# Attention over 120 keys in two layers: masked keys in place of masked queries, and values and sums of a head from one product, joined by VectorE's block transposes

## The reference, cut to what matters

```python
q, k, v = layernorm(x) @ Wq, ctx @ Wk, ctx @ Wv      # split in 16 heads of 8
scores = q . k / sqrt(8) + mask or bias
out = softmax(scores) @ v                            # [128, 16*8]
x = x + tanh(g) * (out @ Wo)
```

## Time and profile before

| | |
|---|---|
| median of 3 runs | 961.47 us (961.18 to 963.21) |
| the profiled execution | 967.42 us |
| its span | 965.7 us |
| mean granted TensorE clock | 0.911 of full speed |
| TensorE busy | 772.4 us, 80% of the span |
| VectorE busy | 689.2 us, 71% |
| GpSimd busy | 614.8 us, 64% |
| ScalarE busy | 494.7 us, 51% |

### The profile page before, as it was taken

One profiled execution on the slowest core, in us unless ns is written; L12 is line 12 of the kernel. 1 busy time (PEld: TensorE's weight loads), 2 busy tenths in 40 slices (PEclk: granted clock), 3 DMA queues, 4 the chain that ended last, 5 costly groups with the idle time before them and its releaser, 6 DMA issues. The chain is left out here.

```text
span 965.7 us, 30722 instructions
## 1 busy us (share of the span) xinstructions
PE 772.4 (80%) x9843; PEld 590.3 (61%) x9843; DVE 689.2 (71%) x2096; ACT 494.7 (51%) x1719; POOL 614.8 (64%) x1114
## 2 busy tenths in 40 slices
PE   3999999999957998369999999999930278888770
PEld 2777777777743666247777778778720146657560
DVE  3788888888866664157888888888869756775334
ACT  2777777777740212047877877777710032342320
POOL 4888666666643676467877877777410266777772
PEclk9999999999977999579999999999965579999995
DMA  6111222222113333134333443343200225665567
GB/s 173 60 64 63 85 76 73 73 73 73 72 60 94 101 103 99 46 99 132 122 111 125 138 129 113 126 138 122 78 15 0 65 49 139 180 183 160 163 187 217
DMA packets 98743, 100.83 MB, mean 104 GB/s; under 512 B 24510, under 2 KB 76076, under 8 KB 98658
## 3 DMA queue, kind: packets, MB, share of 16 engines
q1 hardware_dynamic: 88306, 88.25, 29.4%
q0 software_dynamic: 6656, 9.66, 3.7%
q10 hardware_dynamic: 3696, 1.84, 0.7%
HBM read 60.84 MB, written 44.17 MB: 109 GB/s over the span
## 5 line engine op out<-in xcount | busy, mean ns | idle before, releaser
L558 ACT ACTIVATE P<-bank,mx 128x120 f32<-128x120 f32 x1024 | 278.1, 436 | 12.9 <-DVE mx L849 12.4
L460 PE MATMUL bank<-ident,P 128*120 128x128 f32 x1024 | 166.4, 285 | 12.2 <-ACT P L558 9.1
L849 DVE TENSOR_REDUCE mx<-bank 128x4 f32<-128x480 f32 x256 | 150.3, 649 | 18.2 <-PE bank L447 15.3
L460 PEld LDWEIGHTS bank<-ident,P 128*120 128x120 f32 x1024 | 106.0, 137 | 58.0 <-issue 29.1
L1695 POOL DMA_INDIRECT xg<-token_rows,tokens x64 | 66.3, 1036 | 71.0 <-DVE tokens L1749 52.1
L476 PE MATMUL bank<-PT,Vb 120*32 120x128 f32 x2048 | 105.9, 279 | 0.0
L476 PE MATMUL bank<-PT,headcols 120*32 120x128 f32 x2048 | 102.8, 273 | 0.0
L437 PE MATMUL bank<-bp,identr 128*128 128x480 f32 x256 | 87.3, 427 | 0.0
L1705 POOL DMA_INDIRECT expert_sums<-y,sum_rows x64 | 72.2, 1129 | 23.4 <-issue 18.9
L660 POOL TENSOR_TENSOR Qm<-qf,qmask 128x512 f32<-128x512 f32 x64 | 67.4, 1054 | 27.5 <-ACT qf L542 26.7
L624 POOL TENSOR_SCALAR rs<-mv 128x1 f32<-128x1 f32 x128 | 28.9, 226 | 84.6 <-DVE mv L831 84.3
(11 more groups left out here) (245 smaller groups left out, 1819.3 us busy)
## 6 DMA issues: line engine op xcount, KB each, us to landing
expert_sums<-zeros SPq DMA_DIRECT2D x32, 512.0 KB, 3.4
choice_rows<-zeros SPq DMA_DIRECT2D x32, 384.0 KB, 2.4
yrows<-choice_rows SPq DMA_DIRECT2D x32, 384.0 KB, 3.2
XT<-expert_sums SPq DMA_DIRECT2D x16, 512.0 KB, 6.6
XS<-expert_sums SPq DMA_DIRECT2D x16, 512.0 KB, 6.1
w<-in_w13T SPq DMA_DIRECT2D x8, 704.0 KB, 4.1
token_rows<-payload SPq DMA_DIRECT2D x32, 128.0 KB, 1.7
ctx<-in_ctxT SPq DMA_DIRECT2D x64, 60.0 KB, 1.9
```

The lines of the kernel that those rows point to most:

```text
L460: mm = nc.tensor.transpose(TB[r % 2][0:KV, S * j:S * j + S], t.P[:, r, j, :], t.ident[:])
L558: e = nc.scalar.activation(t.P[:, r, j, :], heads(SC[r])[:, j, :], ACT.Exp, bias=t.mx[:, G * r + j:G * r + j + 1], scale=-1.0)
L849: ve.tensor_reduce(t.mx[:, G * r:G * r + G], heads(SC[r]), AX.X, ALU.min).then_inc(ev.mins, 1)
```

## The change

1. Masked keys. GpSimd now makes four copies of the keys (`head_keys`, tile `Km`, 128x480) and not of the queries, and the queries are the weights. One product per row group gives all four heads of the group, 480 columns wide. ScalarE copies `Kf` ahead of `qf`.
2. Values and sums together. A head's weights are nine columns: its 8 values and a column of ones, in a slot of 16. Two heads (32 columns) fill one row group of PSUM, so values and sums of 16 heads stand in `pv_ps`, now 256 columns. `headcols` and its products are gone.
3. VectorE turns `pv_ps` in blocks of 32x32 (`turn_values`) into `ov`, where the sums of the 16 heads are 16 columns; inverts these 16 (`invert_sums`), multiplies (`divide`, both inputs in SBUF) and turns the result back (`turn_back`) into `oT`.
4. The statistics of the batch three ahead are split in two helpers, and with the choice (layer 0) or the addition of the experts' rows (layer 1) put between the four steps of 3.
5. `BEHIND` is 4 in both layers: while layer 0 drains, its choice comes one step earlier, with the second norm.

```diff
-AHEAD, BEHIND = 4, (5, 4)
+AHEAD, BEHIND = 4, 4
...
+def with_ones(v):
+    return v.rearrange("p v g (r x) -> p (v g r) x", x=48)
+def draining(i, ahead=0):
+    return isinstance(i, int) and i >= B + 1 - ahead
...
             def scores(b, u):
-                for j in range(G):
-                    for r in range(G):
-                        rows = slice(32 * r, 32 * r + 32)
-                        mm = nc.tensor.matmul(heads(SC[r])[:, j, :], t.Qm[rows, u, j, :], t.Kf[rows, u, :],
-                                              start=False, stop=(j == G - 1))
+                for r in range(G):
+                    rows = slice(32 * r, 32 * r + 32)
+                    nc.tensor.matmul(heads(SC[r]), t.qf[rows, u, :], t.Km[rows, u, :, :],
+                                     start=False, stop=True).then_inc(ev.scores, 1)
...
-                for out, col in ((pv_ps, None), (sum_ps, t.headcols)):
-                    for j in range(G):
-                        w = t.Vb[0:KV, v, j, 32 * r:32 * r + 32] if col is None else col[0:KV, r, :]
-                        mm = nc.tensor.matmul(out[32 * j:32 * j + 32, :], w,
-                                              t.PT[0:KV, r, S * j:S * j + S], start=(r == 0 and col is None),
-                                              stop=(r == G - 1), skip_group_check=True)
+                for j in range(G):
+                    mm = nc.tensor.matmul(pv_ps[32 * j:32 * j + 32, S * (r // 2):S * (r // 2) + S],
+                                          t.Vb[0:KV, v, 2 * j + r // 2, 32 * (r % 2):32 * (r % 2) + 32],
+                                          t.PT[0:KV, r, S * j:S * j + S], start=(r % 2 == 0), stop=(r % 2 == 1),
+                                          skip_group_check=True)
...
-            def head_queries(n, w):
-                nc.gpsimd.tensor_tensor(t.Qm[:, w, :, :], t.qf[:, w, :].unsqueeze(1).broadcast_to([D, G, S]),
+            def head_keys(n, w):
+                nc.gpsimd.tensor_tensor(t.Km[:, w, :, :], t.Kf[:, w, :].unsqueeze(1).broadcast_to([D, G, KV]),
...
-            def invert_sums(p, u, c):
+            def turn_values(p, c):
                 dve.wait_ge(ev.pv, G * (p + 1))
-                c.note(ve.reciprocal(t.rsum[:], sum_ps))
-            def normalise(p, u, c):
+                used(dve, ev.out, p)
+                c.note(ve.transpose(t.ov[:].rearrange("p (q h x) -> p h q x", h=2, x=32), pv_ps))
+            def invert_sums(c):
+                c.settle()
+                c.note(ve.reciprocal(t.rsum[:].unsqueeze(2), sixteen(t.ov)[:, :, DK:DK + 1]))
+            def divide(c):
+                c.settle()
+                c.note(ve.tensor_tensor(t.on[:].rearrange("p (g d) -> p g d", d=DK), sixteen(t.ov)[:, :, 0:DK],
+                                        t.rsum[:].unsqueeze(2).broadcast_to([128, 16, DK]), ALU.mult))
+            def turn_back(p, u, c):
                 c.settle()
                 used(dve, ev.proj, p - 1)
-                scaled = ve.tensor_tensor(t.oT[:, u, :], pv_ps, t.rsum[:], ALU.mult)
-                scaled.then_inc(ev.out, 1)
+                ve.transpose(t.oT[:, u, :], t.on[:]).then_inc(ev.out, 1)
```

143 lines of the change are left out of this document (88 added, 55 removed).

## The result

| | before | changed |
|---|---|---|
| device time, median | 962.34 us (961.18 to 971.79, 4 runs) | 940.41 us (935.60 to 943.52, 4 runs) |
| profiled execution | 967.42 us, span 965.7 | 940.70 us, span 938.9 |
| TensorE's granted clock over the span, share of 2.4 GHz | 0.911 | 0.903 |

The ratio of the times is 0.9744, 95% interval 0.9702 to 0.9785: the changed kernel is 2.6% faster. The forecast was 928.5 us in a range of 914 to 944, so the time lies inside the range, 12 us above the forecast. The two profiled executions differ by 26.7 us, the sum of the prediction was 33.

The account below looks back on a forecast made before the run. Layer 0 was taken as bound by two near-equal loops closing in the scores (ScalarE's exponentials; sums to `oT`), layer 1 by VectorE's string; 11.9 + 17.2 + 1 + 3 = 33 us, from the 961.5 us median 928.5, range 914 to 944.

Parts of the forecast that it names:

- Layer 0: Layer 0's step: with `oT` early, TensorE waits for ScalarE; 7.50 us against 7.94, saving 0.44 x 27 = 11.9 us.
- scores to turn: Scores stage on TensorE: four products of 480 columns take 0.95 us to the next turn, before 1.10; -0.15 us.
- The four VectorE instructions: VectorE's transpose, reciprocal, division, transpose back: 0.45, 0.24, 0.29, 0.30 us, sum 1.28 against 1.25 removed; only waiting changes.
- VectorE's string: Layer 1: VectorE's run of instructions bounds the step; shortening it saves 0.66 us per step, to 8.15, 17.2 us in all.
- the "better" rival: Layer 1: experts' addition never meets GpSimd's long product, period falls to GpSimd's 7.85; sum 41, 920 us; chance 0.06.
- GpSimd is behind both and neither ends last: 0: Small parts: `head_keys` waits for `Kf`, `qf` follows one instruction later; GpSimd follows both, neither ends last; cost 0.
- The ends: Ends of the layers: nine further steps save about 0.35 each, 3 us; layer 0's dropped last step 1 us.
- The drain: End of layer 0: loses its last step, but remaining steps carry more in line; between 0 and 2.7, taken 1 us.
- the first rival: Layer 1 gives little: division and transposes contend with GpSimd, period stays at 8.6, 942 us; chance 0.17.
- The passes of a wide product: Scores: second passes block the next row group, five passes, 2.1 us; layer 0 step 8.65, 974 us; chance 0.05.
- dear: VectorE's transposes cost 0.96 us per 128 columns, +2.1 us on VectorE, 1028 us; chance 0.02.
- The clock: TensorE, with 0.9 us less per step, falls to 1.2 GHz at times, losing part of the gain; 0.02, shared with other causes.

Follow-up runs that it names:

- the added copy: The changed kernel with one more 128x512 ScalarE copy per step of both layers, its result unread; ratio 1.0034 to the kernel before.
- the second set of products back: The changed kernel with a second set of four products per group, weights zero, giving TensorE back the removed products; 949.28 us, 0.9831 of the kernel before.

## Why the prediction was right, and where it was off

**Layer 0: right, and for the reason given.** The prediction had 7.50 us, with ScalarE late next; the loop runs at 7.50, and ScalarE's idle time fell from 1.70 to 1.25 us as said. The single terms were a little off and cancel: scores to turn 1.02 and not 0.95; from a turn to the end of that step's last exponentials it is 6.11 us as before (180.76 to 184.65 + 2.22 = 186.87); and to the last mask 0.05 and not 0.15. That ScalarE's part of the loop has no slack is shown by the added copy, which arrives in full. Of the 0.48 us per step the masked keys make 0.06 to 0.08 (two experiments, 0.15 predicted), and the sums product that is gone 0.10. What is left, about 0.3, I put down to the earlier `oT`, from transposes and a narrow reciprocal; no run takes these back alone, so that part is argued.

**The four VectorE instructions: right.** Predicted 0.45, 0.24, 0.29 and 0.30 us, measured 0.441, 0.243, 0.274 and 0.311. The Trainium skill (VectorE: DVE Perf Modes, The three transpose paths) gives 311 ns for a 128x128 transpose in bf16; the trace has the same 311 ns, although the data here are full precision. VectorE did not get less work, and the gain lies in the waits: with the four in a row layer 1 gives back 0.32 of its 0.53 us.

**Layer 1: the mechanism half right, the end wrong.** The step that failed is the one that ran the whole layer along VectorE's string to 8.15 us. The string did shrink as worked out: transpose to next copy is 553.39 - 551.62 = 1.77 us, against a predicted 1.85. But the period stopped at 8.25, because another loop is longer than what is left of the string. I had read it in layer 0 and not worked it out for layer 1: from the exponentials' start at 548.89 to their end at 553.95 ScalarE has 5.06 us, then come 0.19 to the bias, 0.61 for its two passes, 1.02 for the scores, 0.75 to the copy and 0.59 to the next exponentials at 557.11, together 8.22. That is layer 0's loop with a bias in two passes and slightly longer small parts. Four experiments show it: a third transpose on VectorE costs nothing, taking 0.4 us off VectorE gives nothing, 0.50 us more on ScalarE cost 0.51, and scores that take 0.08 us longer cost 0.06. No run lengthened GpSimd's string. Against the forecast 0.13 us per step are missing: 0.53 over the sixteen periods, where I had 0.66. From first to last residual it is -15.2 us, where 17.2 and some of the ends' 3 had been promised.

Even that much owes something to luck. I worked the 0.66 out from one step of 8.65 us, of the kind of which three in four are. Those fell from 8.58 on the mean to 8.21, by 0.37. The fourth fell from 9.71 to 8.49, by 1.22: in it the addition of the experts' rows took 1.23 us before (at 605.61, where the steps before and behind have 0.60) and takes 0.48 now. That is what the "better" rival had described, and it made up for part of what the string did not give.

**"GpSimd is behind both and neither ends last: 0": wrong at one place, right in the rest.** The keys' product is ready 0.5 us before the scores in layer 1 (554.28 against 554.75), and GpSimd then idles 0.60 us (up to 555.72). But in steps 6 and 7 it also clears `xp`, and the scores then stand for 2.14 us with the clock down behind them. The step that takes 11.21 us had taken 9.52 before, so the fault was there in the kernel before (a wait of 1.46 us with the clock at 1.00) and grew by 1.7 us. With the second set of products back the step takes 9.88 at a clock of 1.00, so about 1.2 us of the growth go with the clock and the rest with the longer wait. I had read one step of each layer, not the outlier among the 31. It eats 3.5 us of the changed kernel (11.21 - 7.75).

**The ends: 3 + 1 us, too much.** The drain was to give 1 us since it has a step less; it costs 1 us, since each remaining step has more in line, which the prediction named and took too cheaply. Beside the gap before, 288.6 - 276.0 = 12.6 us from last residual to `tile_count`, the changed kernel has 13.1. How much of the 3 us for the ends came can't be told from the step at 80 us and the long fourth steps; both together are in the sum below.

**The rivals.** Contention on the division, the first rival, is there but small: the median is 0.274 us, and only two of 64 take longer than 0.35 (0.64 and 0.83). So layer 1 gave less than forecast, as that rival had it, but not for its reason. The addition of the experts' rows got out of it, 0.311 us at the median after 0.594, as the "better" case had hoped. In layer 0 the choice (L944) moved into it instead: 0.160 us before, now

```profile
L944 DVE TENSOR_TENSOR sel<-marked,biased x32: 182/406/501, 60.2 to 275.4; 128x64 f32<-128x64 f32 x32
```

because it now meets GpSimd's masked product, for a shape half as wide: the 23 that overlap with `Km`'s row have a median of 0.41 us, and of the nine others eight take 0.18 to 0.23. It costs nothing there, since VectorE has slack. The Trainium skill (GPSIMD Engine Reference, Specifications, the entry on SBUF interfaces) names contention with VectorE instructions that have two SBUF inputs, and these rows agree. The passes of a wide product do not stand in line: eight passes take 1.09 us. The transposes, at 0.44 and 0.31 us, are not dear either. The clock, for which I saw little, cost about 1.2 us: it was down for some 3.4 us behind the wait at 80 us. Otherwise it was down in the attention layers only as they start (layer 1) and drain, in both kernels.

**The sum.** Forecast -33 us, measured -26.7 between the profiled executions and -21.9 between the medians. Of the 6.3 us missing in the traces, 6.9 are in the two layers from first to last residual (25.2 where 11.9 + 17.2 + 3 = 32.1 were promised), with the step at 80 us and the early end of layer 1's gain in them. Another 1.3 are missing between the layers (+0.3 where the drain was to give 1), and 1.8 came behind the last residual, where nothing had been promised. The other 5 us are how the executions scatter: the profiled one of the kernel before stands 5.1 us above its median, that of the changed kernel 0.3 us above its own, and the forecast had been set off the median of before.

The whole time would not have decided it. The 940.4 us lie inside the range, but nearer to the first rival's 942 than to the forecast's 928.5. It is the periods, 7.50 and 8.25 against the rival's 8.6 in layer 1, that speak for the forecast's mechanism as far as it holds.

**A version that is probably faster still.** Clearing `xp` where GpSimd has nothing urgent gives 0.9712 of the kernel before; on the same chip the third transpose, which has the changed kernel's own periods, gives 0.9756. The intervals of the two ratios overlap, but layer 0 is 4.2 us shorter between its first and last residuals, with a cause that can be seen.

## What to carry to other kernels

When the string of one engine is shortened, work out in advance the length of every other loop of the step; the period is the longest of them, and the gain ends there. A drain with fewer steps is not a shorter drain if what the step carried moves into a chain. The first kernel to try is one with an instruction added to the suspected engine: if the period does not grow by the whole of it, the bound is elsewhere. And count the periods one by one before reading a "typical" step: the one step that takes nearly half as long again costs as much as a tenth of a microsecond in each of the others.

Filling the waits of dependent instructions with work that was waiting anyway gave more than half of the gain in one layer and nothing in the other, since it only counts on the engine that closes the loop. Products in different row groups should start together: three cost what four do, and a split stage costs double.

## What was not expected of the hardware

- A 128x512 copy of ScalarE shows 0.71 us in its row, but costs 0.50 us in the period.
- One full-precision product of 480 columns in one row group takes as long, 1.07 us with its two passes, as three or four such products in different row groups (1.08 and 1.09).
- A wait of 2.14 us on TensorE was followed by a stretch at a granted clock of 0.65, in which four turns took 1.11 us and not 0.65. The wait thus cost more than itself. With the second set of products in the kernel a wait of 2.01 us at the same place was followed by a stretch at 1.00, and the step took 9.88 us instead of 11.20.
- A VectorE product of 128x64 with both inputs in SBUF took 0.18 to 0.23 us apart from GpSimd's masked product and 0.41 us at the median where the two overlapped.
- The same kernel, the one before, took 962 and 966 us in the first two sets of runs and 1032 and 1035 us on the second and third chip. It was not profiled there; the third transpose, on the second chip, has the changed kernel's periods in the attention layers and needs 31 us more between the layers (196.2 after 165.2) and 36 more behind the last residual (294.2 after 257.9). Why the blocks of experts are slower there stays open.
